# A routed two-layer block on one core: the second half's attention, its router and several helper steps put earlier in each engine's program

## The chip, the cores and the metric

The kernel runs on one core of one Trainium2 chip. The metric is the device time of one execution in microseconds (us); the number that counts is the median of several runs. A change of about 1% is the least that a measurement of this kernel can tell from no change.

## The reference

The input x has 4 sequences of 256 rows with 256 features; ctx has 4 x 256 x 64. Four residual steps follow one another, each on a layer-normalised copy:

```python
x = x + tanh(g_xattn[0]) * attn0(layernorm(x), ctx)       # sim = x' (kv'kv) with its own norm, softmax over 256
x = x + tanh(g_ffn[0])   * ffn0(layernorm(x))             # top-1 of 32 masked ternary 256x256 weights, times its probability
x = x + tanh(g_xattn[1]) * attn1(ctx, layernorm(x))       # top 76 of 256 of sim(ctx), sigmoid, symmetrised, mixed with x
x = x + tanh(g_ffn[1])   * ffn1(layernorm(x))             # 64 experts of width 64, top 8, plus a shared expert
```

In `attn0`, `ffn0` and `ffn1` each row depends on itself (and on ctx) alone. In `attn1` the 256 x 256 matrix of each sequence is added to its transpose, and this needs all 256 thresholds of the sequence.

## The kernel before

The 1024 rows are 8 tiles of 128 rows (t = 0..7), in two halves h = 0, 1 of four tiles. Each engine has a program that is written out by hand in a fixed order; semaphores tie them together. An engine that waits holds everything that stands behind the wait in its own program. VectorE is "DVE", ScalarE "ACT", GpSimd "POOL", SyncE "SP" and TensorE "PE" in the rows.

Front part (to about 123 us of the profiled execution), per half:

- `similarity`, `scale_rows`, `similarity_rows`, `softmax_rows`, `attend`: the first attention. `attend(h)` adds its result to X and asks GpSimd for the root of the variances (`rsqrt(r, n)`: POOL computes `rstd` for request r; each request is answered at its fixed place in POOL's program). `attended(h)` takes the answer.
- `router_x` (PE transposes), `router_rows` (ACT copies), `router(h)` (PE products), `choose(h)` (DVE top-1), `ranks`, `assign_spares`, `owners`, `assign_owners`, `owners_of`, `assign_slots`: every row gets a slot in a table of 12 x 128 rows, 32 rows an expert; an expert with more rows gets spare places. `set_owners(h)` writes which expert owns each of 15 spares.
- `scatter(h)` (POOL, indirect DMA) writes the rows to slots in DRAM, `load_rows(h)` (ACT's DMA queue) brings them back in expert order. `load_spares(h)` (SP) copies the owner's weights to each spare place: per spare one `value_load` of the owner's number and one DMA.
- `routed_x(h, p)` (PE transposes), `routed_rows(h, p)` (ACT copies to xT), `experts(h, p)` (PE), `expert_rows(h, p)` (ACT copies), `store_rows(h, p)` (DMA), for p = 0..5. Then `gather(h)` (POOL) brings each row its result, `weigh_rows` (ACT) weighs it and `add_rows` (POOL) adds it to X.
- Meanwhile DVE works through `find(n)`: n steps of a search for the 76th largest value of each row of `SIM`. A tile takes 19 steps (`MAX8` and `MATCH_REPLACE8` in turn), eight tiles 152. When a tile is through, `adjacency(t)` makes the thresholded matrix. `mask_weights(m)` multiplies the 32 masks into ternary weights, in 8 pieces.
- `rows_stats`, `rows_ask(0)` (request 4), `rows_affine(0)`, `mix_rows(0)` (ACT), `symmetric(0, k)` (PE: matrix plus transpose), `rows_mix(0)`, `rows_moments(0)` (request 5), `rows_normalise(0)`: the second attention of half 0 and the norm after it. `prep_x3t(0)`, `prep_logits(0)`, `top_find(0)`, `top_weigh(0)`, `prep_wt(0)`, `first_weights` make ready the last layer.
- `high_half(q)` (ACT) and `low_half(q)` (POOL) split the fp32 weights of expert pair q into two fp16 halves. `keep_busy(n)` gives PE n matmuls whose result nobody reads.

Main part: for half 0 and then half 1, one shared step and 32 pair steps (n = 0..32, and NS = 33 on). A step is `project` (12 matmuls of 512 columns), `silu_step`, `gate_step`, `weigh_step`, `high_step`, `low_step`, `down` (12 matmuls of 256 columns). Half 0's loop has half 1's later work in it at fixed values of n: `rows_stats` to `rows_normalise(1)`, `symmetric(1, k)`, `prep_x3t(1)`, `prep_logits(1)`, `lows(1)`, `top_find(1)`, `top_weigh(1)`, and at n = 32 `prep_wt(1)`. `final(h)` adds the accumulated result to X after the last `down` of a half, and SP writes it out.

## Time and profile before

| | us |
|---|---|
| median of 3 runs | 409.98 |
| lowest and highest | 407.95, 410.47 |
| the profiled execution's own time | 406.02 |
| its span, first to last instruction | 404.3 |
| TensorE matmul busy (share of the span) | 358.7 (89%) |
| VectorE busy | 272.6 (67%) |
| ScalarE busy | 181.1 (45%) |
| GpSimd busy | 163.0 (40%) |
| mean granted TensorE clock, share of full | 0.947 |

The span is read in three stretches: the front part up to about 123 us, where the engines wait for one another; half 0's loop of steps up to 268 us; half 1's loop to the end. The profiled execution is 3.96 us below the median.

### The profile page before, as it was taken

The numbers are of one execution on the slowest core, as the hardware profiler recorded it, in microseconds if no ns is written. First come the engines' busy times: TensorE is split into PE (matmuls) and PEld (weight loads), VectorE is DVE, ScalarE is ACT, GpSimd is POOL, SyncE is SP. The second block draws the span as 40 slices with busy tenths as digits, with TensorE's granted clock in tenths as the row PEclk, the third lists the DMA queues.
The fourth block names the chain that finished last, engine by engine and source line by source line (L and its number), as shares of the span: only waits on it lengthen the run. The fifth ranks groups of instructions, "written<-read, shape, count | busy, mean of one in ns | idle before, by whom it ended". The sixth has DMA issues, their size and how long they took to land. (4 is left out here: it accounts for less than half of the span.)

```text
span 404.3 us, 7694 instructions
## 1 busy us (share of the span) xinstructions
PE 358.7 (89%) x2419; PEld 217.4 (54%) x2419; DVE 272.6 (67%) x711; ACT 181.1 (45%) x354; POOL 163.0 (40%) x180
## 2 busy tenths in 40 slices
PE   8987928643977899999899999969999999999995
PEld 2755426312644365546466666645665656656563
DVE  3999896999376585999784484557555555555454
ACT  3477736624744446544645446533323233332331
POOL 6937542437551349978699677220000000000000
PEclk9996967785999899999999999999999999999999
DMA  7899964686701444445355442004121221212211
GB/s 186 139 258 218 197 208 149 221 263 217 233 17 51 128 137 131 130 131 195 132 190 174 159 153 73 25 29 146 61 78 58 72 71 58 78 56 74 77 53 52
DMA packets 50346, 51.31 MB, mean 127 GB/s; under 512 B 6732, under 2 KB 41484, under 8 KB 50318
## 3 DMA queue, kind: packets, MB, share of 16 engines
q1 hardware_dynamic: 34430, 38.08, 30.0%
q0 software_dynamic: 9216, 6.29, 9.1%
q10 hardware_dynamic: 6672, 6.59, 5.1%
q8 instruction: 14, 0.23, 0.2%
q14 instruction: 14, 0.11, 0.1%
HBM read 44.13 MB, written 7.08 MB: 127 GB/s over the span
## 5 line engine op out<-in xcount | busy, mean ns | idle before, releaser
L1047 PE MATMUL bank<-early,gu 128*128 128x512 f16 x768 | 177.7, 381 | 3.0 <-DVE arena L1608 3.0
L1047 PEld LDWEIGHTS bank<-early,gu 128*128 128x128 f16 (+1 forms) x768 | 75.0, 98 | 83.0 <-issue 4.4
L499 ACT ACTIVATE arena<-arena 128x512 f16<-128x512 f32 (+1 forms) x66 | 41.6, 631 | 134.6 <-DVE arena L1624 133.8
L1074 PE MATMUL bank<-dp,arena 128*128 128x256 f16 (+1 forms) x768 | 94.2, 273 | 1.1 <-POOL arena L457 0.7
L1074 PEld LDWEIGHTS bank<-dp,arena 128*128 128x128 f16 x768 | 74.7, 98 | 23.5 <-POOL arena L457 2.7
L1608 DVE TENSOR_TENSOR arena<-arena,bank 128x512 f32<-128x512 f32 x64 | 43.9, 686 | 56.7 <-PE bank L1047 40.2
L457 POOL TENSOR_TENSOR arena<-arena 128x512 f16<-128x512 f32 (+1 forms) x33 | 38.3, 1161 | 51.1 <-ACT arena L499 51.1
L1624 DVE TENSOR_TENSOR arena<-arena,early 128x512 f32<-128x512 f32 x64 | 48.4, 756 | 7.5 <-DVE arena L1608 2.7
L740 ACT ACTIVATE arena<-bank 128x512 f32<-128x512 f32 (+1 forms) x66 | 38.7, 588 | 17.5 <-PE bank L1047 17.4
L406 POOL TENSOR_TENSOR gu<-stage,gu 128x512 f16<-128x512 f32 x32 | 39.0, 1219 | 7.4 <-ACT dp L499 7.4
L1634 DVE TENSOR_TENSOR arena<-arena 128x512 f16<-128x512 f32 (+1 forms) x33 | 22.8, 691 | 24.5 <-ACT arena L499 24.5
L1206 DVE MAX8 t<-work 128x8 f32<-128x256 f32 x72 | 30.7, 426 | 2.0
L795 PE MATMUL bank<-ones 128*128 128x512 f16 x97 | 26.5, 420 | 1.8 <-DVE ones L1508 1.1
L407 POOL TENSOR_TENSOR dp<-stage,dp 128x256 f16<-128x256 f32 x32 | 27.5, 859 | 0.0
L1211 DVE MATCH_REPLACE8 work<-t,work 128x256 f32<-128x256 f32 x64 | 26.1, 408 | 0.0
L499 ACT ACTIVATE gu<-stage 128x512 f16<-128x512 f32 x32 | 19.7, 617 | 0.7 <-ACT arena L499 0.5
L975 PE MATMUL bank<-gu 128*32 128x256 f16 x256 | 12.0, 344 | 7.7 <-ACT gu L499 7.7
L795 PEld LDWEIGHTS bank<-ones 128*128 128x128 f16 x97 | 9.3, 104 | 16.0 <-issue 7.4
L499 ACT ACTIVATE arena<-bank 128x512 f32<-128x512 f32 (+1 forms) x18 | 10.7, 595 | 12.9 <-PE bank L975 7.0
L399 POOL TENSOR_TENSOR rstd<-var_in,minus_half 128x4 f32<-128x4 f32 x8 | 8.2, 1026 | 18.5 <-DVE var_in L1247 17.0
L1233 DVE BATCH_NORM_STATS2 bn<-X 128x6 f32<-128x256 f32 x32 | 11.8, 413 | 5.2 <-DMA X<-in_x 5.2
L420 POOL DMA_INDIRECT routed_rows<-arena,slot x8 | 10.1, 1265 | 8.9 <-DVE slot L1397 7.1
(184 smaller groups left out, 368.6 us busy)
## 6 DMA issues: line engine op xcount, KB each, us to landing
early<-token_weights SPq DMA_DIRECT2D x126, 128.0 KB, 2.9
stage<-in_gu_t SPq DMA_DIRECT2D x32, 256.0 KB
gu<-in_masks_t POOLq DMA_DIRECT2D x16, 256.0 KB, 22.5
stage<-in_dp_t SPq DMA_DIRECT2D x32, 128.0 KB
expert_rows<-arena ACTq DMA_DIRECT2D x12, 256.0 KB
dp<-gu SPq DMA_DIRECT2D x22, 128.0 KB, 2.3
routed_rows<-arena SPq DMA_DIRECT2D x1, 1536.0 KB, 17.5
arena<-routed_rows ACTq DMA_DIRECT2D x3, 512.0 KB, 5.1
```

Source lines behind the costliest of these rows:

```text
L406: nc.gpsimd.tensor_tensor(gu16[:, q, 1, :, :], stage_gu[s], gu16[:, q, 0, :, :], ALU.subtract)
L407: nc.gpsimd.tensor_tensor(dp16[:, q, 1, :], stage_dn[s], dp16[:, q, 0, :], ALU.subtract).then_inc(lo_ready, 1)
L457: nc.gpsimd.tensor_tensor(inter16[0:m, s, 1, :], inter[0:m, s, :], inter16[0:m, s, 0, :], ALU.subtract).then_inc(ilo_ready, 1)
L499: return nc.scalar.activation(dst, src, ACT.Copy, scale=scale)
L740: nc.scalar.activation(silu[0:m, s, :], ps_gate[s][0:m, :], ACT.Silu).then_inc(silu_ready, 1)
L795: mm(dst.rearrange("p (a b) -> p a b", a=4), ones16[:, :], ones16[:, None, :].to_broadcast([P, 4, P]), start=True, stop=True)
L1047: last = mm(dst[:, :], w, x16[:, h, b, c, :], start=(k == 0), stop=(k == 3 * C - 1))
L1074: last = mm(dst, inter16[0:m, s, a, k * P:(k + 1) * P], w, start=(q is None and j == 0 and k % 2 == 0), stop=True, skip_group_check=True)
L1206: last = steps(v.max(t8[:, t, :], src))
L1211: last = steps(v.match_replace(work[:, :], t8[:, t, :], src, NEG))
L1608: v.tensor_tensor(gated[0:m, s, :], silu[0:m, s, :], up, ALU.mult).then_inc(gated_ready, 1)
L1624: v.tensor_tensor(inter[0:m, s, :], gated[0:m, s, :], row, ALU.mult).then_inc(inter_ready, 1)
```

## The change

No operation of the computation is added or dropped; the program of every engine is reordered at some places. In words: on DVE `similarity_rows(1)` stands ahead of the mask products and `attend(1)` right behind them, and search steps are dealt out otherwise; on PE `router_x((2, 3))` and `router(1)` stand ahead of or behind the first expert group, the last transpose of it goes to another bank, `symmetric(0, 0)` stands among half 1's experts, and `keep_busy` counts change; on ACT `weigh_rows` of half 0 stands behind half 1's first two `routed_rows`, `load_rows(1)` ahead of two `high_half`; on POOL `rsqrt(4)` and `rsqrt(5)` stand ahead of `low_half`; SP reads all 15 owners before it waits for the masks; `rows_mix` and `rows_moments` of half 0 are merged tile by tile (`rows_mixed`); in half 0's loop `lows(1)`, `prep_logits(1)`, `top_find(1)` and `top_weigh(1)` come one step sooner; `final(1)` starts on two tiles when their bank is done.

```diff
@@ load_spares (SP)
                 sp.wait_ge(owner_set, h + 1)
+                owner = [sp.value_load(spare_e[0:1, h, j:j + 1], min_val=0, max_val=E0 - 1) for j in range(SPARE)]
                 sp.wait_ge(mask_ready, MB)
-                for j in range(SPARE):
-                    e = sp.value_load(spare_e[0:1, h, j:j + 1], min_val=0, max_val=E0 - 1)
+                for j, e in enumerate(owner):
@@ gpsimd
-            for q in range(4, 7):
-                low_half(q)
             rsqrt(4, HT)
+            low_half(4)
+            low_half(5)
+            rsqrt(5, HT)
+            low_half(6)
+            gather(1)
             low_half(7)
-            rsqrt(5, HT)
-            gather(1)
@@ scalar
+            softmax_rows(1)
             load_rows(0)
-            softmax_rows(1)
             routed_rows(0, 0)
             routed_rows(0, 1)
+            router_rows(1)
             expert_rows(0, 0)
             routed_rows(0, 2)
             store_rows(0, 0)
+            norm_rows(1, 4, 5)
...
+            load_rows(1)
             high_half(4)
             high_half(5)
-            load_rows(1)
-            weigh_rows(0, 1, 2, 3)
             routed_rows(1, 0)
             routed_rows(1, 1)
+            weigh_rows(0, 1)
             expert_rows(1, 0)
+            weigh_rows(2, 3)
...
             prep_rows(0)
             top_rows(0)
+            silu_step(0, 1, I1)
             prep_weights(0)
-            silu_step(0, 1, I1)
...
-                if n == 27:
+                if n == 26:
                     prep_rows(1)
-                if n == 30:
+                if n == 29:
                     top_rows(1)
@@ tensor
-                        pe.wait_ge(xnt_copied, 3)
+                        pe.wait_ge(sim_used, HT)
...
+                    if isinstance(n, int) and n == 2 * NS - 1 and k == HT // 2 - 1:
+                        last.then_inc(bank_done, 1)
...
+            symmetric(0, 0)
             experts(1, 0)
...
-            keep_busy(10, bank[0][:, :])
-            symmetric(0, 0)
+            keep_busy(6, bank[0][:, :])
             symmetric(0, 1)
-            keep_busy(14, bank[0][:, :])
+            keep_busy(24, bank[0][:, :])
             prep_x3t(0)
...
-                if n == 29:
+                if n == 28:
                     prep_logits(1)
@@ vector
-            find(2)
+            find(5)
             assign_spares(0)
             find(1)
             assign_owners(0)
             assign_slots(0)
             set_owners(0)
+            similarity_rows(1)
             for m in range(2, MB):
                 mask_weights(m)
-            similarity_rows(1)
+            attend(1)
             weights_of_rows(0)
-            find(4)
-            attend(1)
-            find(3)
+            find(2)
             attended(1)
-            find(6)
+            find(7)
             choose(1)
...
             thresholds(2)
+            find(2)
             rows_affine(0)
-            rows_mix(0)
-            rows_moments(0)
+            rows_mixed(0)
             find(3)
             rows_normalise(0)
...
+            def rows_mixed(h):
+
+                r = asked[0]
+                asked[0] += 1
+                rows_mark[1] = r
+                tiles = tiles_of(h)
+                done = {}
+                for t in tiles:
+                    rows_mix(h, t)
+                    done[t] = rows_mark[0]
+                    if t > tiles[0]:
+                        steps.need(done[t - 1])
+                        done[t - 1] = steps(moments(X[:, t - 1, :], t - 1))
...
+                dve.wait_ge(bank_done, 1) if h else dve.wait_ge(down_ready, NS)
                 for k in range(HT):
                     t = HT * h + k
+                    if h and k == HT // 2:
+                        dve.wait_ge(down_ready, 2 * NS)
...
-                if n == 27:
+                if n == 26:
                     lows(1)
+                if n == 29:
+                    top_find(1)
                 if n == 30:
-                    top_find(1)
-                if n == 31:
                     top_weigh(1)
```

On PE, the first expert groups of half 0. L896/L899 are `router_x`, L908/L911 `router`, L951/L954 `routed_x`, L975/L978 `experts`. Before:

```order
32 L951 MATMUL bank<-ident,arena 128x128 x16
33 L975 MATMUL bank<-gu 32x256 x32
34 L951 MATMUL bank<-ident,arena 128x128 x8
35 L975 MATMUL bank<-gu 32x256 x32
36 L951 MATMUL bank<-ident,arena 128x128 x8
37 L896 MATMUL bank<-ident,X 128x128 x8
38 L975 MATMUL bank<-gu 32x256 x32
39 L951 MATMUL bank<-ident,arena 128x128 x8
40 L908 MATMUL bank<-router_c,xn_t 128x32 x8
```

After:

```order
32 L954 MATMUL bank<-ident,arena 128x128 x16
33 L899 MATMUL bank<-ident,X 128x128 x8
34 L978 MATMUL bank<-gu 32x256 x32
35 L954 MATMUL bank<-ident,arena 128x128 x8
36 L911 MATMUL bank<-router_c,xn_t 128x32 x8
37 L978 MATMUL bank<-gu 32x256 x32
```

The router's transposes moved ahead of the first expert group, and its products ahead of the second.

On POOL, behind `add_rows` of half 0. L399/L400 is `rsqrt`, L406/L407 and L407/L408 the two instructions of `low_half`, L429/L430 `gather(1)`. Before:

```order
48 L406 TENSOR_TENSOR gu<-stage,gu 128x512
49 L407 TENSOR_TENSOR dp<-stage,dp 128x256
50 L406 TENSOR_TENSOR gu<-stage,gu 128x512
51 L407 TENSOR_TENSOR dp<-stage,dp 128x256
52 L406 TENSOR_TENSOR gu<-stage,gu 128x512
53 L407 TENSOR_TENSOR dp<-stage,dp 128x256
54 L399 TENSOR_TENSOR rstd<-var_in,minus_half 128x4
55 L406 TENSOR_TENSOR gu<-stage,gu 128x512
56 L407 TENSOR_TENSOR dp<-stage,dp 128x256
57 L399 TENSOR_TENSOR rstd<-var_in,minus_half 128x4
```

After:

```order
48 L400 TENSOR_TENSOR rstd<-var_in,minus_half 128x4
49 L407 TENSOR_TENSOR gu<-stage,gu 128x512
50 L408 TENSOR_TENSOR dp<-stage,dp 128x256
51 L407 TENSOR_TENSOR gu<-stage,gu 128x512
52 L408 TENSOR_TENSOR dp<-stage,dp 128x256
53 L400 TENSOR_TENSOR rstd<-var_in,minus_half 128x4
54 L407 TENSOR_TENSOR gu<-stage,gu 128x512
55 L408 TENSOR_TENSOR dp<-stage,dp 128x256
56 L430 DMA Z<-expert_rows,slot 128x256 x4
```

The first root moved ahead of three weight halves, the second ahead of two, so that one half now stands right behind it.

On ACT, at the start of half 1's experts. L615/L617 is `load_rows(1)`; `Z<-Z,tiny` is `weigh_rows`, `gu<-bank` is `routed_rows`, `arena<-bank` is `expert_rows`. Before:

```order
76 L615 DMA early<-routed_rows 128x4x512 x3
77 L499 ACTIVATE Z<-Z,tiny 128x256 x4
78 L499 ACTIVATE gu<-bank 128x1024 x2
79 L499 ACTIVATE arena<-bank 128x512
80 L499 ACTIVATE gu<-bank 128x1024
```

After:

```order
77 L501 ACTIVATE gu<-bank 128x1024 x2
78 L501 ACTIVATE Z<-Z,tiny 128x256 x2
79 L501 ACTIVATE arena<-bank 128x512
80 L501 ACTIVATE Z<-Z,tiny 128x256 x2
81 L501 ACTIVATE gu<-bank 128x1024
```

The copies that feed half 1's experts moved ahead of the weighing.

## Rows read from the trace of the kernel before

**Rows 1.** TensorE's waits over the whole span: us in total, times, longest.

```profile
PE bank L975 <- ACT gu L499: 7.9, 3, 6.3
...
PE bank L1023 <- DVE Z L1496: 4.4, 2, 3.2
```

**Rows 2.** Chain that ended last, half 1's loop: start us, us, what.

```profile
274.50 1.31 PE bank L1074 x12
275.81 2.59 PE bank L1047 x12
```

**Rows 3.** VectorE's waits in 38 to 119 us.

```profile
DVE mix L1441 <- POOL rstd L399: 5.9, 1, 5.9
DVE lg L1349 <- PE bank L908: 3.7, 1, 3.7
DVE X L1452 <- PE bank L996: 2.0, 2, 1.1
DVE spares L1367 <- PE bank L925: 1.4, 1, 1.4
```

**Rows 4.** VectorE's timeline, front part: start us, us, what, idle before it.

```profile
44.20 11.02 DVE L1504 TENSOR_TENSOR gu<-gu,tern 128x1024 f16<-128x1024 f16 x12
...
98.61 0.41 DVE L1233 BATCH_NORM_STATS2 bn<-X 128x6 f32<-128x256 f32 x1
...
103.39 0.24 DVE L1433 TENSOR_SCALAR var_in<-mv 128x4 f32<-128x4 f32 x1
...
110.91 0.23 DVE L1441 TENSOR_SCALAR mix<-rstd,k_mix 128x4 f32<-128x4 f32 x1 [5.91 <-POOL rstd L399]
...
116.90 0.17 DVE L1247 TENSOR_SCALAR var_in<-mv 128x4 f32<-128x4 f32 x1
...
118.31 1.46 DVE L1283 TENSOR_SCALAR XN<-X,mv,rstd 128x256 f32<-128x256 f32 x4
```

**Rows 5.** Costliest groups, the search steps: busy, mean ns, idle before.

```profile
L1206 DVE MAX8 t<-work 128x8 f32<-128x256 f32 x72 | 30.7, 426 | 2.0
...
L1211 DVE MATCH_REPLACE8 work<-t,work 128x256 f32<-128x256 f32 x64 | 26.1, 408 | 0.0
```

**Rows 6.** GpSimd's timeline: a weight half, and the root for request 4.

```profile
100.70 1.16 POOL L406 TENSOR_TENSOR gu<-stage,gu 128x512 f16<-128x512 f32 x1
...
109.83 1.05 POOL L399 TENSOR_TENSOR rstd<-var_in,minus_half 128x4 f32<-128x4 f32 x1
```

**Rows 7.** TensorE's timeline, end of the front part.

```profile
114.00 3.19 PE L795 MATMUL bank<-ones 128*128 128x512 f16 x14
119.08 1.40 PE L1006 MATMUL bank<-ident,XN 128*128 128x128 f32 x8 [1.90 <-DVE XN L1283]
...
133.40 4.22 PE L1047 MATMUL bank<-early,gu 128*128 128x512 f16 x12 [1.26 <-DVE arena L1608]
```

**Rows 8.** ScalarE's timeline.

```profile
84.03 0.60 ACT L499 ACTIVATE arena<-bank 128x512 f32<-128x512 f32 x1 [3.68 <-remote]
...
111.46 2.08 ACT L540 ACTIVATE Z<-X,mix 128x256 f32<-128x256 f32 x4 [1.92 <-DVE mix L1444]
...
130.60 1.28 ACT L740 ACT_TABLE_LOAD   x1
```

**Rows 9.** SyncE's DMA issues: spare weights of half 0, then token weights.

```profile
56.23 18.58 SPq L285 DMA_DIRECT2D dp<-gu  x15
...
131.95 4.99 SPq L332 DMA_DIRECT2D early<-token_weights  x8
```

**Rows 10.** Line L1504, all instructions: duration ns min/median/max.

```profile
L1504 DVE TENSOR_TENSOR gu<-gu,tern x16: 683/685/4402, 21.6 to 50.8; 128x1024 f16<-128x1024 f16 x16
```

**Rows 11.** VectorE's timeline, half 1's normalisation beside GpSimd's work.

```profile
236.99 3.06 DVE L1283 TENSOR_SCALAR XN<-X,mv,rstd 128x256 f32<-128x256 f32 x4 [0.31 <-POOL rstd L399]
```

**Rows 12.** Timelines at `prep_wt(1)` and at the end.

```profile
267.35 0.65 PE L1023 MATMUL bank<-ident,Z 128*65 128x128 f32 x4 [3.20 <-DVE Z L1496]
...
400.16 1.66 DVE L1641 SCALAR_TENSOR_TENSOR X<-bank,tg,X 128x256 f32<-128x256 f32 x4 [1.58 <-PE bank L1074]
```

More of the change, by code:

```diff
@@ L193, in flamingo_block @@
         ps_x3t = [bank[0], bank[7]], [bank[2], bank[1]]
-        ps_xr = [bank[1], bank[3], bank[1], bank[1]]
+        ps_xr = [bank[1], bank[3], bank[1], bank[7]]
         ps_down = [bank[0], bank[7]]
@@ L248, in flamingo_block @@
         logits1_copied = sem("logits1_copied")
+        bank_done = sem("bank_done")
         x_d = x.rearrange("b s d -> (b s) d").rearrange("(t p) d -> p t d", p=P)
@@ L664, in _ @@
             store_rows(0, 1)
-            router_rows(1)
-            norm_rows(1, 4, 5)
+            norm_rows(1, 6, 7)
             expert_rows(0, 2)
@@ L669, in _ @@
             store_rows(0, 2)
-            norm_rows(1, 6, 7)
+            router_exp(1)
             expert_rows(0, 3)
@@ L703, in _ @@
             store_rows(1, 3)
-            high_half(6)
             expert_rows(1, 4)
@@ L709, in _ @@
             mix_rows(0)
+            high_half(6)
             high_half(7)
@@ L1114, in _ @@
             routed_x(0, 1)
+            router_x((2, 3))
             experts(0, 0)
             routed_x(0, 2)
+            router(1)
             experts(0, 1)
             routed_x(0, 3)
-            router_x((2, 3))
             experts(0, 2)
             routed_x(0, 4)
-            router(1)
             experts(0, 3, 0)
@@ L1453, in rows_mix @@
                                                                 ALU.mult, ALU.add))
+            def rows_mixed(h):
[10 more added lines that the diff above has]
+                        done[t - 1] = steps(moments(X[:, t - 1, :], t - 1))
+                steps.need(done[t])
+                done[t] = steps(moments(X[:, t, :], t))
+                for t in tiles:
+                    steps.need(done[t])
+                    m = steps(v.bn_aggr(mv[:, t, :], bn[:, t, :]))
+                steps.need(m)
+                v.tensor_scalar(var_in[:, r, :], mv[:, HT * h:HT * h + HT, 1], 1.0, EPS, ALU.mult, ALU.add
+                                ).then_inc(var_ready, 1)
             def rows_normalise(h):
```

2 lines of the change are left out of this document (removed).

## The prediction

> **What bounds the kernel now.** I read TensorE's waits first, then the chain that ended last, then VectorE's waits and its timeline over the front part. From 123 us on TensorE is nearly always busy: a step of half 1's loop is 2.59 us of projection and 1.31 us of down, 3.90 us together, and the chain runs through these alone [rows 2]. No edit touches that pace. What can be won is waiting: one wait of 3.20 us in the middle, where TensorE needs the token weights of half 1 (`prep_wt(1)`) [rows 12], the tail behind the last matmul, and the front part, whose end is the start of the steps. TensorE's largest single wait in front is 6.3 us for ScalarE [rows 1], but to end it is worth nothing by itself, for what ends the front part is VectorE: TensorE waits 1.90 us for the normalised rows at 119.08 although it has 3.19 us of filler just ahead [rows 7]. So the front part is costed on VectorE. From 44.20 on it has masks, search steps and norms without a hole until 98.61, except where rows 3 say so: 1.4 us for the ranks, 3.7 for the router's logits, 5.9 for the root of request 4 and 2.0 for the symmetric products, 13.0 us together [rows 3, 4].
>
> **Half 0's ranks.** Three more search steps stand ahead of `assign_spares(0)`. A step is 0.43 or 0.41 us plus a short value load, about 0.49 as they follow one another [rows 5], so 1.4 us of wait become 1.4 us of work: gain 1.4. The slots come 0.1 to 0.2 late, taken as nothing.
>
> **Second router sooner.** With `similarity_rows(1)` (about 1.6 us) ahead, the masks start near 46.0 and end near 57.0 in place of 55.2 [rows 4]. `attend(1)` follows at once, so its rows stand in X at 59.1, some 2 us sooner than before. TensorE, which then has just transposed the first routed rows, transposes X (0.6 us a group) and starts the experts about when it did before; the logits come near 65.4. VectorE reaches `choose(1)` at about 65.7: the 3.7 us are gone. The new wait is for `ranks(1)`: three expert groups stand ahead of it on TensorE, so it ends near 69.9 and VectorE, there at 69.1, waits some 1.1. Net gain 2.6. Slots of half 1 near 73.4, before 77.4.
>
> **Spare owners.** Fifteen loads with their register reads take 18.58 us, 1.24 each; plain issues of this queue take 4.99 for eight, 0.62 each [rows 9]. Read ahead, the copies of half 0 take some 9.3 us behind the masks and end near 67, ahead of the need at about 72. For half 1 the reads can't hide, because the owners come near 74.5 and the masks are long done: 9.3 of reads, 9.3 of copies, landing at about 96. Half 1's experts need them at 96 to 97. Worth nothing here on the path, and a wait of up to 1 us on TensorE is covered, since ScalarE's mix isn't wanted before 103.
>
> **Gather, weighing, and half 1's experts.** The results of half 0 are stored near 77, gathered from about 80 and added to X by about 93; VectorE, with the same search work to do, comes to `rows_stats(0)` only at about 95 (98.61 before [rows 4]), so the moved `weigh_rows` costs nothing; the cover is 2 us. Half 1's experts start near 88 in place of 97.9 and are through at about 99.5, ahead of the mix.
>
> **GpSimd's root first.** The request goes out at 103.39, the root starts at 109.83, since `low_half(6)` stands ahead and waits for a ScalarE copy that stands behind the experts [rows 4, 6]. Put first, it answers 1.05 us after the request. VectorE meanwhile has four search steps and a threshold matrix. Gain 5.9.
>
> **Symmetric products and merged mix.** The first product is done among the experts, the second by 103.4. Then ScalarE sets the pace: 2.08 us for four tiles [rows 8]. From the affine step to the request for root 5 it was 110.91 to 116.90, 6.0 us [rows 4]; now I get 4.5. Gain 1.5 of the 2.0.
>
> **Sum in front.** 1.4 + 2.6 + 5.9 + 1.5 = 11.4. Two more search steps stand ahead of `rows_normalise(0)` than before (81, not 79): minus 1.0. This gives 10.4; a walk through the timeline by durations gives 9.9 to 10.4, with the normalised rows near 108.5 and the longer filler (24 instructions for 14, some 5.2 us at the rate of 3.19 for 14 [rows 7]) ending about then.
>
> **What VectorE and GpSimd do to each other.** One mask product took 4.40 us where the median is 0.69: it lasted through two weight halves of GpSimd [rows 10]. Half 1's normalisation took 3.06 us for four tiles beside GpSimd's work, half 0's took 1.46 [rows 4, 11]. The new order brings such neighbours: the choice of half 1 beside `low_rows`, the matrix of tile 2 beside `add_rows`, the affine step beside `low_half(4)` and `(5)`, and above all `rows_normalise(0)` right beside `low_half(6)`, which was done before. From below nothing, from above 1.6 (normalise, 3.06 less 1.46) plus one stall of 3.7 (4.40 less 0.69). I take 1.1 for normalise, since its first tiles meet one or two of those instructions, and 1.3 for the other three together: minus 2.4. Front gain **8.0**. The Trainium skill, "SBUF — State Buffer", Who interferes with whom, says that a VectorE instruction with two SBUF inputs, or one in a two-port mode, and a GpSimd instruction that reads SBUF exclude each other, and that the later one blocks for the other's whole instruction. By that rule each of the four meetings would cost up to one GpSimd instruction of 1.16 us, 4.6 in all, and the front would gain 5.8; the 4.40 us row shows more than one instruction's worth in one stall, so the trace agrees with the exclusion and not with its length.
>
> **Start of the steps.** `silu_step(0)` now pays its table load of 1.28 us [rows 8] while ScalarE had been waiting for the transposed weights. Its silu is ready some 2.5 us sooner, the weights copy 0.4 later, and the step that started at 133.40 after a wait of 1.26 [rows 7] can start behind `first_weights`, at 132.6: gain 0.8. That step took 4.22 us, against 2.59 for the same work, at a granted clock of 1.2 GHz in part; if the shorter hole holds 2.4 GHz, 1.6 more. I leave this out, as a hole of 1.2 us remains.
>
> **Middle.** Everything from `prep_logits(1)` to `top_weigh(1)` comes one step, 3.9 us, sooner; 1.75 us of logits only change places. `top_weigh(1)` then ends near 263.4, TensorE is there at 264.1: gain **3.2**, with 0.7 to spare. What is late next is nothing, the token weights shift along. `prep_rows(1)` one step sooner holds `silu_step(27)` until the transposes are copied, about 4 us; the double buffer has room for one step, so none is charged; without it 1 us.
>
> **Tail.** Two tiles of `final(1)` run while TensorE does the last six matmuls. `final` was 1.66 us [rows 12] behind the last matmul, now half of it; the outputs are issued one after the other, so 0.65 is gained. Extra wait instruction: none that shows.
>
> **Sum.** 8.0 + 0.8 + 3.2 + 0.65 = 12.65. The profiled execution took 406.02, so 393.4 by its own time; it lies 3.96 under the median of 409.98, against which the forecast is 409.98 - 12.65 = **397.3 us**.
>
> **Rivals.**
> - Full gain: no stall between VectorE and GpSimd, and the clock holds in the first step. Front 10.4, start 2.4, so 16.65 gained: 393.3. For it: search steps ran at 0.43 beside weight halves. Against: rows 10 and 11. Chance 0.17.
> - The gather chain takes VectorE's place. ScalarE sat 3.68 us before the last expert copy of half 0 on something that no engine of this core explains [rows 8]; if that stays and transfers (gather, rows of half 1, spare copies) crowd one another, X is complete near 99 instead of 93, and the front gains 4 less: 401.3. The Trainium skill, "DMA: Bandwidth & Descriptors", Issuing engines are not separate DMA queues, says that all queues share the same engines; no row here separates what each lost. Chance 0.20.
> - The longer filler is the bound: 24 matmuls at 1.2 GHz take 10.3 us instead of 5.2, and the transposes wait for them, 4 to 5 us: 401.8. It needs a clock that fell in the 1.7 us hole ahead of the second product; the hole of 1.90 us before 119.08 [rows 7] left it at full speed. Chance 0.07.
> - The order does not do what it says: VectorE's freed waits come back behind another, such as the mask products, and only the middle and tail gain, 3.85: 406.1. Chance 0.04.
> - Slower: TensorE starts the steps at 1.2 GHz and stays there, as the half step at 133.40 did for a while [rows 7]. Every step would cost 3.9 us more; past 3.3 steps the whole gain is gone, at five it is 397.3 + 19.5 = 416.8. Against it: the next projection of the same length in the trace is back at its full pace of 2.59, and so are all behind it [rows 2]. Chance 0.02.
>
> The forecast itself has 0.50. The range reaches from the full gain to the two cases near 401.5, with 1 us on the low and 2 on the high side for what the median itself moves: 392.3 to 403.5. A time of under 405.9 is faster by over 1%; that holds for all but the last two cases and some luck of the median: faster 0.92, within 1% 0.05, slower 0.03.
>
> **What would show it.** VectorE: no wait for the root and none for logits, about 1 us for ranks, `rows_normalise(0)` starting at 108 to 111. TensorE: the first `prep_x3t` 7 to 10 us sooner, no wait at L1023's successor near 260 us, 3.90 a step as before. SyncE: copies 0.62 apart. GpSimd: the first root straight behind its request. Wrong it would be if VectorE showed a new wait for `rows_added`, or the transposes started behind the filler.

## The result, and the profile after

| | before | after |
|---|---|---|
| median | 410.23 (407.95 to 411.04, 4 runs) | 393.28 (392.48 to 394.04, 4 runs) |
| ratio, 95% interval | | 0.9595 (0.9549 to 0.9642) |
| the profiled execution's own time, span | 406.02, 404.3 | 392.48, 390.7 |
| mean granted TensorE clock | 0.947 | 0.965 |

The changed kernel is faster, and 393.28 lies inside the range of 392.3 to 403.5, 4.0 below the forecast of 397.3. The forecast was a gain of 12.65 us, made from one execution; the same execution pair gained 13.54. The medians, 16.95 apart, gained more than either trace. The unaltered changed kernel, measured a second time (told below), gave 11.2 us by medians and a ratio of 0.9675 (0.962 to 0.9731), which is 13.2 of 407.39; ratios here leave out a kernel's runs that lie more than 1.5% above its fastest. So the gain that this pair of traces supports is 13.5. What the medians add or take away is at least in part the clock, below; the later measurements were also made on three different chips, and no run here separates chip from execution.

To compare traces I cut each span at TensorE's own rows: the first product of `ranks(0)`, the first transpose of `prep_x3t(0)`, the projection behind `first_weights`, the first down step, `prep_wt(1)`, and the last down step. "Front" is from the first of these to the second, and so on; the tail is what is left of the span.

| | ranks at | front | start | first projection | half 0 | half 1 | tail | span |
|---|---|---|---|---|---|---|---|---|
| before | 40.41 | 78.67 | 14.32 | 4.16 | 129.79 | 131.29 | 5.65 | 404.3 |
| after | 41.17 | 69.12 | 13.33 | 2.69 | 127.22 | 132.22 | 4.99 | 390.7 |
| difference | +0.76 | -9.55 | -0.99 | -1.47 | -2.57 | +0.93 | -0.66 | -13.6 |

VectorE's waits in the front part after the change (columns: what waited for what, us in total, times, longest), the answer to [rows 3]:

```profile
DVE X L1457 <- ACT Z L542: 0.7, 1, 0.7
```

The waits for ranks, logits and the root are gone altogether; of 13.0 us one of 0.7 is left. VectorE's timeline shows what that bought (columns: start, duration, operation, and in brackets the idle time before it and what ended it), against [rows 4]:

```profile
99.69 0.17 DVE L1438 TENSOR_SCALAR var_in<-mv 128x4 f32<-128x4 f32 x1
...
102.01 0.26 DVE L1446 TENSOR_SCALAR mix<-rstd,k_mix 128x4 f32<-128x4 f32 x1
102.31 0.59 DVE L1448 SCALAR_TENSOR_TENSOR mix<-mv,mix 128x4 f32<-128x4 f32 x1
...
103.64 0.98 DVE L1457 SCALAR_TENSOR_TENSOR X<-bank,k_mix,Z 128x256 f32<-128x256 f32 x2 [0.67 <-ACT Z L542]
...
107.03 0.17 DVE L1479 TENSOR_SCALAR var_in<-mv 128x4 f32<-128x4 f32 x1
...
108.42 2.47 DVE L1288 TENSOR_SCALAR XN<-X,mv,rstd 128x256 f32<-128x256 f32 x4
```

The request for root 4 goes out at 99.69 instead of 103.39, the affine step is at 102.0 instead of 110.91, the request for root 5 at 107.03 instead of 116.90, and the normalised rows start at 108.42, inside the 108 to 111 that was forecast. They take 2.47 us, not 1.46 as in [rows 4]. GpSimd's timeline shows the neighbour:

```profile
99.94 1.05 POOL L400 TENSOR_TENSOR rstd<-var_in,minus_half 128x4 f32<-128x4 f32 x1 [4.88 <-DVE var_in L1438]
...
107.28 1.01 POOL L400 TENSOR_TENSOR rstd<-var_in,minus_half 128x4 f32<-128x4 f32 x1 [2.65 <-DVE var_in L1479]
108.26 1.14 POOL L407 TENSOR_TENSOR gu<-stage,gu 128x512 f16<-128x512 f32 x1
109.37 0.71 POOL L408 TENSOR_TENSOR dp<-stage,dp 128x256 f16<-128x256 f32 x1
```

Both roots now start within 0.25 us of their request, and `low_half(6)` runs while VectorE normalises: 1.01 us too much, where the sum had 1.1.

TensorE's timeline, against [rows 7, 12]:

```profile
103.14 5.34 PE L798 MATMUL bank<-ones 128*128 128x512 f16 x24
110.29 1.32 PE L1009 MATMUL bank<-ident,XN 128*128 128x128 f32 x8 [1.80 <-DVE XN L1288]
...
119.98 0.65 PE L1026 MATMUL bank<-ident,Z 128*65 128x128 f32 x4 [1.32 <-DVE Z L1523]
121.65 1.07 PE L1062 MATMUL bank<-early,ident 65*64 65x512 f32 x2 [1.02 <-ACT early L501]
...
123.62 2.76 PE L1050 MATMUL bank<-early,gu 128*128 128x512 f16 x12
...
180.73 2.75 PE L1050 MATMUL bank<-early,gu 128*128 128x512 f16 x12 [0.68 <-DVE arena L1634]
...
253.53 0.60 PE L1026 MATMUL bank<-ident,Z 128*65 128x128 f32 x4
...
265.45 1.48 PE L1077 MATMUL bank<-shared_dn,arena 64*128 64x256 f16 x12 [0.91 <-DVE X L1669]
```

The reader is to see four things. The transposes (L1009) come at 110.29 instead of 119.08, 8.8 us sooner, and still wait for VectorE with an idle hole ahead. The projection at 123.62 took 2.76 where its counterpart took 4.22. `prep_wt(1)` at 253.53 has no bracket any more: the 3.20 us are gone. And two waits are new, 0.68 at 180.73 and 0.91 at 265.45, neither of which the prediction had.

SyncE's timeline, against [rows 9]:

```profile
58.11 11.53 SPq L286 DMA_DIRECT2D dp<-gu  x15
...
83.25 5.10 SPq L286 DMA_DIRECT2D arena<-gu  x8
88.49 4.44 SPq L286 DMA_DIRECT2D dp<-gu  x7
```

Fifteen spare copies of half 0 take 11.53 us, 0.77 each, not the 0.62 of plain issues and not 1.24. Half 1's fifteen, in the two lower rows, take 9.7 together.

### The profile page after: what moved, and what is told of

It is laid out like the page before. It is cut to its first block and busy times, and to the rows that moved or that the text cites. A ratio compares the mean times of both kernels' runs of the same rounds, so it can differ in the third digit from the quotient of the medians.

```text
span 390.7 us, 7704 instructions
## 1 busy us (share of the span) xinstructions
PE 357.3 (91%) x2425; PEld 219.2 (56%) x2425; DVE 275.5 (71%) x711; ACT 179.8 (46%) x354; POOL 162.2 (42%) x180
## 5 line engine op out<-in xcount | busy, mean ns | idle before, releaser
L407 POOL TENSOR_TENSOR gu<-stage,gu 128x512 f16<-128x512 f32 x32 | 39.0, 1219 | 0.0
L408 POOL TENSOR_TENSOR dp<-stage,dp 128x256 f16<-128x256 f32 x32 | 27.5, 859 | 0.0
L400 POOL TENSOR_TENSOR rstd<-var_in,minus_half 128x4 f32<-128x4 f32 x8 | 8.2, 1026 | 24.4 <-DVE var_in L1252 15.4
L501 ACT ACTIVATE gu<-bank 128x1024 f16<-128x1024 f16 x12 | 12.1, 1021 | 10.0 <-PE bank L954 8.3
L1531 DVE TENSOR_TENSOR gu<-gu,tern 128x1024 f16<-128x1024 f16 x16 | 13.6, 914 | 0.9 <-DMA gu<-in_masks_t 0.9
```

What stands on the lines that cost most here:

```text
L407: nc.gpsimd.tensor_tensor(gu16[:, q, 1, :, :], stage_gu[s], gu16[:, q, 0, :, :], ALU.subtract)
L408: nc.gpsimd.tensor_tensor(dp16[:, q, 1, :], stage_dn[s], dp16[:, q, 0, :], ALU.subtract).then_inc(lo_ready, 1)
L501: return nc.scalar.activation(dst, src, ACT.Copy, scale=scale)
```

## The experiments

Twelve runs follow: eleven variants, and the changed kernel once more (after_again). Times are medians; the ratio is to the kernel before, run beside it. The medians of the kernel before in the four measurements were 410.23, 411.15, 407.23 and 407.39, so kernels of different measurements are compared by ratio or stretch by stretch. The columns from "front" on come from one profiled execution of each, cut as above.

| | time | ratio (95%) | front | start | first | half 0 | half 1 | span |
|---|---|---|---|---|---|---|---|---|
| changed kernel | 393.28 | 0.9595 (0.9549 to 0.9642) | 69.12 | 13.33 | 2.69 | 127.22 | 132.22 | 390.7 |
| u_root | 395.6 | 0.9624 (0.9578 to 0.967) | 70.70 | 13.48 | 4.17 | 127.21 | 132.31 | 394.4 |
| u_spares | 401.55 | 0.9793 (0.9732 to 0.9854) | 76.54 | 13.33 | 2.69 | 127.25 | 132.18 | 398.8 |
| u_silu | 397.25 | 0.9665 (0.9611 to 0.9718) | 69.34 | 14.41 | 4.92 | 127.25 | 132.42 | 396.3 |
| u_middle | 397.31 | 0.9695 (0.9623 to 0.9768) | 68.91 | 13.33 | 2.69 | 130.57 | 132.97 | 395.9 |
| b_root | 410.55 | 1.0071 (1.0027 to 1.0114) | 77.49 | 14.42 | 5.08 | 129.76 | 132.82 | 405.6 |
| x_gather | 395.96 | 0.9732 (0.9647 to 0.9817) | 67.88 | 15.73 | 4.67 | 127.20 | 132.35 | 394.3 |
| x_final | 393.86 | 0.9665 (0.9583 to 0.9748) | 68.85 | 15.13 | 3.99 | 127.85 | 131.24 | 394.1 |
| x_filler14 | 394.7 | 0.9695 (0.9618 to 0.9772) | 69.39 | 14.16 | 2.69 | 127.84 | 132.21 | 394.2 |
| after_again | 396.23 | 0.9675 (0.962 to 0.9731) | 70.06 | 15.12 | 3.95 | 127.20 | 132.34 | 395.3 |
| x_busy | 394.42 | 0.9712 (0.9676 to 0.9747) | 69.62 | 13.33 | 2.69 | 128.25 | 132.19 | 392.3 |
| x_calm | 397.64 | 0.9783 (0.9738 to 0.9828) | 68.15 | 17.00 | 5.07 | 127.19 | 132.20 | 395.0 |
| x_best | 395.43 | 0.9679 (0.9618 to 0.974) | 69.54 | 14.90 | 2.68 | 128.13 | 131.23 | 392.2 |

How well a stretch repeats can be read from this table. Six of these kernels are alike up to the first transpose (changed kernel, u_silu, u_middle, x_final, after_again, x_busy), and their fronts are 68.85 to 70.06 long: a difference of about 1 us in the front is hardly more than that spread. Half 1 repeats within 0.3 us where nothing in it was changed and the clock held. Half 0 is 127.2 long in most, but 127.8 to 128.3 in four kernels whose edits lie outside it. By the ratios, of the four edits undone only u_spares lies clear of the changed kernel's interval; the prices of the other three rest on the rows of one profile each.

### Four edits undone, one at a time

**u_root**: GpSimd's root for request 4 behind three weight halves again. `rsqrt(5)` and `gather(1)` stay ahead of `low_half(7)`, which they were not in the kernel before.

```diff
@@ gpsimd, in the changed kernel
+            for q in range(4, 7):
+                low_half(q)
             rsqrt(4, HT)
-            low_half(4)
-            low_half(5)
             rsqrt(5, HT)
-            low_half(6)
             gather(1)
             low_half(7)
@@ scalar
             store_rows(1, 3)
+            high_half(6)
             expert_rows(1, 4)
...
             mix_rows(0)
-            high_half(6)
             high_half(7)
```

> The changed kernel with GpSimd's two roots put back behind the weight halves, and ScalarE's copy for pair 6 back among the experts. Theory A (VectorE's program is what ends the front part, and the root answered late was the largest hole in it): the first root waits for low_half(6), whose ScalarE copy now comes at about 97 us, so the root is done near 103 to 104 in place of 101; a hole of 1 to 2 us on VectorE ahead of the affine step, less some 1 us that normalise wins back without low_half beside it. Span 390.7 + 0 to 1.5, some 391.5. Rival B (the 5.9 us were the root's own, whatever else moves): the hole comes back at 5 to 6 us, span 396.

Measured: the wait for the root is 3.7, between the two theories, and the front is longer by 1.58 only. VectorE's timeline of this kernel:

```profile
105.56 0.23 DVE L1445 TENSOR_SCALAR mix<-rstd,k_mix 128x4 f32<-128x4 f32 x1 [3.68 <-POOL rstd L400]
105.82 0.16 DVE L1447 SCALAR_TENSOR_TENSOR mix<-mv,mix 128x4 f32<-128x4 f32 x1
...
111.51 1.47 DVE L1287 TENSOR_SCALAR XN<-X,mv,rstd 128x256 f32<-128x256 f32 x4
```

With the halves done early nothing of GpSimd's lies beside the affine step (0.16 for 0.59) or the normalise (1.47 for 2.47). So 3.7 of wait bought 1.4 of undisturbed VectorE, and of the price of 1.58 some 1 us lies within the spread of the front. Another 1.5 us is in the first projection, 4.17 for 2.69, and that, as the later runs show, is not to be booked to this edit.

**u_spares**: SyncE reads each owner just before its copy again.

```diff
@@ load_spares (SP), in the changed kernel
-                owner = [sp.value_load(spare_e[0:1, h, j:j + 1], min_val=0, max_val=E0 - 1) for j in range(SPARE)]
                 sp.wait_ge(mask_ready, MB)
-                for j, e in enumerate(owner):
+                for j in range(SPARE):
+                    e = sp.value_load(spare_e[0:1, h, j:j + 1], min_val=0, max_val=E0 - 1)
```

> The changed kernel with each spare owner read just ahead of its copy, as before. Theory A (read ahead is worth nothing of its own): the copies of half 0 take 18.6 us from 58.1, land at 79, TensorE waits 7 us more at the spare experts, but VectorE reaches the row statistics only at 94.9 and absorbs up to 3 us; half 0's rows are complete near 102 in place of 95, so 7 us late, 3 to 5 us on the span: 394 to 396. Rival B (the wait is swallowed by the rest of the front): no change, 390.7 within 0.5.

Measured: the front is 7.42 us longer, by far the largest price of the four. The waits of TensorE and of VectorE and the queue of SyncE in this kernel:

```profile
PE bank L978 <- DMA dp<-gu: 12.6, 2, 9.6
...
DVE spare_e L1408 <- PE bank L939: 7.8, 1, 7.8
...
59.35 20.15 SPq L286 DMA_DIRECT2D dp<-gu  x15
```

The copies take 20.15 us and end at 79.5, TensorE stands 9.61 us in front of `experts(0, 4)` and the product of `owners_of(1)` (L939), 32x16 elements large, stands behind it in TensorE's program; VectorE's `set_owners(1)` waits 7.8 us for that product. In the changed kernel the same place costs TensorE 1.28. Both theories missed: the span is 398.8, beyond the 394 to 396 of theory A, for VectorE absorbed nothing. It comes to `rows_stats(0)` at 103.0 instead of 94.9, since it stood in that wait itself.

**u_silu**: `prep_weights(0)` ahead of `silu_step(0)` again.

```diff
@@ scalar, in the changed kernel
             top_rows(0)
-            silu_step(0, 1, I1)
             prep_weights(0)
+            silu_step(0, 1, I1)
```

> The changed kernel with the copy of the transposed token weights back ahead of the shared silu. Theory A (the table load is hidden in a wait, and the shorter hole keeps TensorE's clock at 2.4 GHz): the second projection starts 0.8 to 1.0 later and takes 4.2 instead of 2.7 us, span 390.7 + 2.4 = 393.1. Rival B (the clock held for another reason, such as the longer filler ahead of it): only the start moves, span 391.6.

Measured: start +1.08 and first projection +2.23. The 1.08 agrees with the 0.8 of the sum. The 2.23 is clock (4.99 us for work that takes 2.75 at 2.4 GHz), and I had taken it as confirmed by this run that the longer hole brings it; after the runs below I do not.

**u_middle**: `lows(1)`, `prep_logits(1)`, `top_find(1)` and `top_weigh(1)` one step later again.

```diff
@@ tensor (the same by one in scalar and vector), in the changed kernel
-                if n == 28:
+                if n == 29:
                     prep_logits(1)
```

> The changed kernel with half 1's logits, top-8 search and weights back at their old steps of half 0's loop. Theory A: TensorE's wait of 3.2 us for the token weights returns, while the wait of 0.9 us for final(0) goes, since the last stretch shifts: span 390.7 + 3.2 - 0.9 = 393.0. Rival B (the 0.9 us wait has nothing to do with it): span 393.9.

Measured: half 0 +3.35, half 1 +0.75. TensorE's timeline shows what happened in half 1:

```profile
257.98 0.65 PE L1026 MATMUL bank<-ident,Z 128*65 128x128 f32 x4 [3.20 <-DVE Z L1523]
258.47 2.34 PE L1077 MATMUL bank<-dp,arena 128*128 128x256 f16 x12
260.60 2.31 PE L1036 MATMUL bank<-early,shared 128*128 128x512 f16 x6
```

The 3.20 us wait is back, to the hundredth. The 0.91 us wait for `final(0)` is gone, for TensorE is later; but the two groups behind the hole ran at 2.34 and 2.31 us instead of 1.47 and 1.46, 1.7 us of clock. In the kernel before the same hole of 3.20 [rows 12] left the clock at full speed: the group behind it took 1.47. A first hint that a hole does not decide by itself.

### The root alone

**b_root**: the kernel before, with GpSimd's part behind `add_rows` in the changed kernel's order (`rsqrt(4)` ahead of `low_half(4)`, `rsqrt(5)` ahead of `low_half(6)`, `gather(1)` ahead of `low_half(7)`) and `high_half(6)` behind `mix_rows(0)`, nothing else.

> The kernel before with one edit: GpSimd answers request 4 ahead of low_half(4) and request 5 ahead of low_half(6), and ScalarE's high_half(6) stands behind mix_rows(0). Theory A (the waits are layered): the 5.9 us wait for the root goes, but half 1's experts of the old order hold TensorE's symmetric products and ScalarE's mix until about 109.6 to 110.5 us, so VectorE waits for them instead; the front is shorter by 1 to 3 us, and the time is about 407 to 409 beside 410 to 411. Theory B (my prediction's sum, in which the root alone was worth 5.9): about 404.5 to 405.

Measured: the front is 1.18 us shorter, and the kernel is not faster at all (ratio 1.0027 to 1.0114). VectorE's timeline:

```profile
105.76 1.13 DVE L1442 TENSOR_SCALAR mix<-rstd,k_mix 128x4 f32<-128x4 f32 x1
...
110.22 0.88 DVE L1453 SCALAR_TENSOR_TENSOR X<-bank,k_mix,Z 128x256 f32<-128x256 f32 x2 [2.63 <-PE bank L997]
111.97 0.88 DVE L1453 SCALAR_TENSOR_TENSOR X<-bank,k_mix,Z 128x256 f32<-128x256 f32 x2 [0.88 <-PE bank L997]
...
116.01 2.14 DVE L1284 TENSOR_SCALAR XN<-X,mv,rstd 128x256 f32<-128x256 f32 x3
```

The affine step is 5.2 us sooner (105.76 for 110.91), the normalise 2.3 (116.01 for 118.31), the transposes 1.2 (117.86 for 119.08). Between them the wait for the symmetric products, which stand behind half 1's experts, grew from 2.0 [rows 3] to 3.5, and two stalls beside weight halves came in, at the affine step and at the normalise. What was left was lost again where the clock fell (first projection 5.08, and 1.5 in half 1, where the transposes behind the 3.19 us hole took 1.12 instead of 0.65). Theory A (layered waits) holds for the front, at the low end of its 1 to 3 us; the gain in time that it still expected did not come.

### Moving GpSimd's weight half out of the way

**x_gather** and **x_calm**:

```diff
@@ gpsimd, x_gather
             rsqrt(5, HT)
-            low_half(6)
             gather(1)
+            low_half(6)
             low_half(7)
@@ gpsimd, x_calm: as x_gather, and
             gather(1)
+            pool.wait_ge(top_ready, 1)
             low_half(6)
```

> The changed kernel with low_half(6) behind gather(1) on GpSimd, so that nothing of GpSimd's arithmetic stands beside rows_normalise(0). Theory A (GpSimd's half blocks VectorE): the four normalising instructions fall from 2.47 us to about 1.46, the transposes start 1.0 sooner, 392.3 by the median. Theory B (their price lies in something else, such as the DMA traffic or ScalarE's copies at 105.98 to 108.6): 2.47 stays and the time stays at 393.3. If GpSimd's indirect DMAs hold VectorE as much, 2.47 or more stays as well.

> The changed kernel with low_half(6) and (7) on GpSimd behind gather(1) and behind a wait for the row maxima (top_ready), so that they stand beside neither rows_normalise(0) nor the four-element scaling in top_find(0), which took 1.47 us in place of 0.34 when low_half(6) was only moved behind gather(1). Theory A: normalise 1.46, the scaling 0.34, transposes 1.0 to 1.3 sooner and the start stretch as in the changed kernel (13.3), so 1.1 less in span at equal clock. Theory B (the stall moves on again, to the expert softmax or the first gate steps): the start stretch grows by 0.7 to 1.2 and nothing is gained.

Measured in x_gather, on VectorE:

```profile
108.41 1.46 DVE L1288 TENSOR_SCALAR XN<-X,mv,rstd 128x256 f32<-128x256 f32 x4
...
115.75 1.47 DVE L1505 TENSOR_SCALAR tiny<-top 128x4 f32<-128x4 f32 x1
```

and in x_calm:

```profile
107.81 1.46 DVE L1289 TENSOR_SCALAR XN<-X,mv,rstd 128x256 f32<-128x256 f32 x4
...
116.01 0.63 DVE L1517 SCALAR_TENSOR_TENSOR Z<-Z 128x64 f32<-128x64 f32 x1
...
117.21 1.18 DVE L1517 SCALAR_TENSOR_TENSOR Z<-Z 128x64 f32<-128x64 f32 x1
```

In both, normalise falls to 1.46, as theory A said of the cause: it is the weight half that made it 2.47. (GpSimd's indirect DMAs ran beside it instead, as in the kernel before, where it took 1.46 too.) But the stall moves. In x_gather it hits a scaling of four elements a row, 1.47 us, which took 0.34 in the changed kernel and 0.17 in x_calm. GpSimd's rows of x_gather show how long it was held: through the rest of one instruction and the whole of the next.

```profile
115.42 1.15 POOL L407 TENSOR_TENSOR gu<-stage,gu 128x512 f16<-128x512 f32 x1
116.53 0.66 POOL L408 TENSOR_TENSOR dp<-stage,dp 128x256 f16<-128x256 f32 x1
```

TensorE's hole ahead of `prep_wt(0)` grows from 1.32 to 2.43 by it, so the front's gain of 1.24 is given back in the start stretch; the rest of what that stretch and the next lost is clock. In x_calm the stall hits the four masked sums of the softmax: 0.63, 0.70, 1.18 and 0.69 where 0.21 to 0.23 is usual, 2.3 us in all, more than the 1.0 that it saved in front, and here too the clock fell behind the longer hole, of 3.11. For the gain at the end, theory B was right in both.

### The wait for final(0)

**x_final**:

```diff
@@ vector, in the changed kernel
             low_step(NS, 0, I1)
-            gate_up(NS + 1, 1)
             final(0)
+            gate_up(NS + 1, 1)
```

> The changed kernel with final(0) ahead of the gate and weigh steps of n = NS + 1 on VectorE. TensorE waited 0.91 us at 265.45 us for final(0), which stood behind two instructions that VectorE could run only late. Theory A: final(0) runs at about 262.4, the 0.91 goes, and the time is 0.9 lower, 392.4. Theory B: what is late is the whole VectorE chain of the shared step (it waited 1.99 us for ScalarE and 0.60 for the token weights' DMA just before), so the wait moves to the down step behind it and the time is unchanged, 393.3.

Measured: half 1 is 131.24 against 132.22, so the wait is gone, 0.98 us, and didn't move to the down steps behind it: theory A. It came from order alone. `final(0)`, whose last input was complete at 261.9 in the changed kernel, stood behind the gate and weigh steps until 263.74. The median did not show the 0.98: this kernel's four times are 395.83, 391.69, 395.75 and 391.96, two pairs 4 us apart. That opened the last question.

### The clock at the first projection

**x_filler14** (24 filler matmuls made 14), **after_again** (the changed kernel, unaltered), **x_busy** and **x_best** (x_busy, x_calm and x_final together):

```diff
@@ tensor, x_busy
             pair_step(0, 0, 0)
+            keep_busy(5, bank[0][:, :])
             prep_wt(0)
+            keep_busy(4, bank[0][:, :])
             first_weights(0, I1)
```

> The changed kernel with keep_busy(14) in place of keep_busy(24) ahead of prep_x3t(0). The filler ends 2.2 us sooner, so TensorE idles about 4.0 us ahead of the transposes instead of 1.80, as it did with the root put back (4.01 us, and the first projection then took 4.17). Theory A (the long filler is what keeps the granted clock through the first projection): the projection at 121.65 or so takes 4.2 instead of 2.7, 1.5 us lost, 394.8. Theory B (the earlier end of the front part, not the filler, did it): the time stays at 393.3.

> The changed kernel, unaltered, as the base for the three variants that run beside it. Theory A (one execution holds the granted clock through the first weights and projections at about 122 us and another doesn't, by chance): its times fall into two groups some 2 to 4 us apart, as an unaltered front part did in the run with final(0) moved (391.7 and 392.0 against 395.8 and 395.8). Theory B: they lie within 1.5 us, as in the first measurement (392.5 to 394.0), and the spread there had come from that variant.

> The changed kernel with five filler matmuls ahead of prep_wt(0) and four behind it, at 0.22 us each, where TensorE had waited 1.32 and 1.02 us. Theory A (the clock at the first projection depends on TensorE's holes just before): the weights' products stay at 1.07 and 1.12 us and the first projection at 2.7 in every execution; the slow group of times goes, and the median is 392 to 393, 1 to 2 below the changed kernel beside it. Theory B (what makes the clock fall lies elsewhere, in the first 110 us): two groups remain, and the median does not move.

> All together: low_half(6) and (7) behind the row maxima (minus 1.1), the fillers around prep_wt(0), and final(0) ahead of the gate step of n = NS + 1 (minus 0.9). Theory A: span 388 to 389, median 389.5 to 391, about 2 to 3 below the changed kernel beside it. Theory B (the gains overlap, or the filler delays what waits for it): above 391.5.

Measured first, the two profiles of one program. x_final's is the changed kernel's up to 262 us. TensorE's timeline in x_final:

```profile
120.59 0.65 PE L1026 MATMUL bank<-ident,Z 128*65 128x128 f32 x4 [1.32 <-DVE Z L1523]
122.26 1.97 PE L1062 MATMUL bank<-early,ident 65*64 65x512 f32 x2 [1.03 <-ACT early L501]
124.16 2.08 PE L1062 MATMUL bank<-early,pick 65*128 65x512 f32 x2
126.03 4.06 PE L1050 MATMUL bank<-early,gu 128*128 128x512 f16 x12
```

The holes ahead, 1.32 and 1.03, are those of the changed kernel's first profile, 1.32 and 1.02. There the weights' products took 1.07 and 1.12 and the projection 2.76. The stretches of the trace by 4 us (columns: window, length, TensorE busy and number of instructions, granted clock, share of the DMA engines, GB/s) say it directly. In x_final:

```profile
120.00:124.00 4.00, 2.39 (x6) 0.73 0.14 37
124.00:128.00 4.00, 4.00 (x8) 0.50 0.31 116
```

and in the first profile of the changed kernel:

```profile
120.00:124.00 4.00, 2.98 (x10) 1.00 0.13 37
124.00:128.00 4.00, 4.00 (x25) 1.00 0.42 152
```

So one program, with the same two holes, is granted 1.2 GHz from about 122 us in one execution and 2.4 in another, and it costs 3.1 us (start 15.13 for 13.33, first 3.99 for 2.69). The two were not alike in all that came before: the hole ahead of the transposes was 0.78 in x_final and 1.80 in the first profile. In the profiled execution of after_again (397.09) that hole is 1.80 too, and what follows is as in x_final: holes of 1.31 and 1.02, products of 1.97 and 2.08, a projection of 4.02. Theory A of after_again holds in that the clock there differs from execution to execution; what decides it is open, and these profiles are of different chips. x_final's four times, on one chip, do lie in two pairs. The "two groups" that theory A named for after_again did not come: the six times are 390.92, 394.11, 395.37, 397.09, 397.73 and 400.77, spread wider than this place explains. Another place is the start: `ranks(0)` came between 40.43 and 42.96 in the kernels of the changed order, whose programs are alike up to there.

x_busy closed the two holes to 0.24 and 0.16 us:

```profile
119.02 1.24 PE L798 MATMUL bank<-ones 128*128 128x512 f16 x5
120.50 0.65 PE L1026 MATMUL bank<-ident,Z 128*65 128x128 f32 x4 [0.24 <-DVE Z L1525]
...
122.17 1.07 PE L1062 MATMUL bank<-early,ident 65*64 65x512 f32 x2 [0.16 <-ACT early L501]
```

Its profile holds the clock, and its six times lie within 2.0 us (394.02 to 396.01), where even the three lowest of after_again span 4.5. That is what theory A said of the spread, with few runs behind it. The gain that it named is not shown: the median is 1.8 below that of after_again's six times, but 0.3 above that of its three lowest, the lowest time is 3.1 above after_again's lowest, and the ratios' intervals overlap (0.9676 to 0.9747 against 0.962 to 0.9731). So it looks steadier, and is not shown to be faster. In its profile half 0 is 1.0 longer, 0.73 of it one new wait for GpSimd at 159 us. Why, is open.

x_filler14 does not decide its question. The first projection took 2.75, not the 4.2 of theory A. The hole ahead of the transposes was 2.99 us, and the clock was down right behind it (0.70 and 0.50 in the windows 112 to 120), with the logits' products at 3.68 instead of 2.00. But u_middle had its clock down at the same place behind the very hole of 1.80 of the changed kernel, so one execution can't be read as an effect of the filler.

x_best: span 392.2, median 395.43, past the 391.5 that theory B named. `final(0)` gave its 1.0 (half 1 131.23), x_calm's stalls took 2.3 as before. There is no version here that is shown to beat the changed kernel. x_calm is shown to be slower: 0.9738 to 0.9828, against 0.962 to 0.9731 for the changed kernel beside it.

## Why the prediction was right, and where it was not

**The total.** Forecast 12.65 from one execution, measured 13.54 from one. Of this 1.47 is the clock of the first projection, which the sum left out; like for like it is 12.65 against 12.1, with 0.8 and 0.2 more than forecast in front and start, and 0.6 and 0.9 less in the two halves. The waits that were to go went, so it is right by mechanism and size, though the price of two single edits in it was wrong. Against the medians the forecast was 4.0 high: the base was the median of before, 4 us above its profiled execution, and the median after was only 0.8 above its own. The step "it lies 3.96 under the median, against which the forecast is 397.3" assumed that this distance is carried over. It isn't a property of the kernel: the changed kernel, measured again, had a median 5.3 above its lowest time. That the median came so far below the forecast is therefore luck.

**Front, forecast 8.0, measured 8.79 of time at the transposes** (9.55 less a start 0.76 later, which no edit explains). The waits for ranks, logits and root went, as said; not even the 1.1 us for `ranks(1)` came. VectorE reached `rows_stats(0)` first at 94.9 (forecast 95). The terms for the ranks (1.4), the second router (2.6) and the merged mix (1.5) were not tried one at a time; they rest on the waits that are gone from VectorE's rows.

**"Gain 5.9" for the root, the step that failed as a price.** Undone in the new order the edit is worth 1.58 in the front, of which the spread of fronts leaves about 1 open; made alone in the old order 1.18, and nothing in the time. The term was right as a piece of a sum in which the symmetric products and half 1's experts were also brought forward, and wrong as the value of the edit.

**"Worth nothing here on the path" for the spare owners: wrong.** By the prediction's own figures the copies without the edit, from about 57 at 1.24 each, would have ended near 75.6, 3.6 past the 72 at which it had them wanted. It asked only whether the copies with the edit are in time, and never priced the new order without it. In the kernel before TensorE waits 1.25 at this place, in u_spares 9.61. VectorE's `set_owners(1)` hangs, through one small product in TensorE's program, on the expert group that needs the spares. Reading ahead holds off 7.42 us. Copies cost 0.77 each, where I had 0.62.

**Start, forecast 0.8: measured 0.99**, and 1.08 when undone. **The first projection**, left out at 1.6, came as 1.47. It was rightly left out: x_final and after_again lack it, with the same program up to there. That it came is luck.

**Middle, forecast 3.2: measured 2.57.** The 3.20 went, and u_middle brings exactly it back. "What is late next is nothing" was wrong twice. At 180.73 TensorE waits 0.68: VectorE's rows show why.

```profile
178.02 1.07 DVE L1448 SCALAR_TENSOR_TENSOR mix<-mv,mix 128x4 f32<-128x4 f32 x1
179.02 0.16 DVE L1449 TENSOR_SCALAR mix<-mix 128x4 f32<-128x4 f32 x1
179.09 0.90 DVE L1234 SCALAR_TENSOR_TENSOR SIM<-SIM,t,XN 128x256 f32<-128x256 f32 x1
```

With the search steps dealt out otherwise, a threshold matrix (L1234) falls into the same step as half 1's affine step, ahead of the gate that TensorE wants; before, it came a step later. The 1.07 of the first row was there in the kernel before too; what is new is the matrix, 0.90 and not its usual 0.48, for it too stood beside a weight half. u_middle has the same wait of 0.68, so it is not from the moved logits and top-8 search. And at 265.45 the wait for `final(0)`, 0.91, took the place of part of the gain. That wait I could have read from the old trace, where `final(0)` ended at 278.05 and its user started at 278.34: it had 0.3 to spare, and the shift used it up (in u_middle, without the shift, the wait is not there).

**Tail, forecast 0.65: measured 0.66.**

**VectorE beside GpSimd, forecast 2.4: measured 2.2.** Normalise lost 1.01 (forecast 1.1). The other three meetings lost 1.2 (forecast 1.3): 0.69 for 0.24 in `assign_spares(1)` beside `low_rows`, 0.82 for 0.48 in the matrix of tile 2, 0.59 for 0.17 in the affine step. The Trainium skill, "SBUF — State Buffer", Who interferes with whom, was weighed there: exclusion for one GpSimd instruction. In x_calm each of the four stalled sums ended within 0.1 us of the end of one GpSimd instruction, which agrees. In x_gather the scaling took 1.47, 1.3 more than alone, and was held through the rest of one instruction and the whole of the next. So this row, like the 4.40 us of [rows 10], agrees with the exclusion and not with its length.

**Rivals.** The full gain (393.3) gives the median almost to the hundredth, for another reason than its own: its stalls-free front did not happen. The gather chain and the clock for good did not come. Nor did the filler: in all eleven profiles of the changed order with 24 of them they took 5.34 us, the rate of the full clock.

## What to carry to other kernels

A wait's length is not an edit's value: where waits are layered, as here, one edit made alone won nothing, and one that was "off the path" was worth 7.4 us once the others were in; cost each edit in the order in which it will run. When a stall between two engines is taken away, ask which instruction stands beside the disturbing one next: here it moved twice. In x_calm it cost 2.3 us on four small sums beside two weight halves, where four large instructions beside one had lost 1.0. When one profiled execution is compared with a median, check first whether the same program's executions differ at one place; here the clock behind a 1 us hole did, by 3 us.

## What the runs showed of the hardware

- Two executions of one program, with holes of 1.32 and 1.02 us in one and 1.31 and 1.02 in the other, were granted 1.00 and 0.50 of the clock right behind them. Holes of 3.20 and 3.19 us left it at full speed in one kernel and not in two others, and a hole of 2.03 left it at full speed in x_best, where one of 1.80 in u_middle did not. No hole length here decides it by itself; with them closed to 0.24 and 0.16 us the one profile taken held the clock.
- GpSimd's weight half delays some VectorE instructions and not others. Beside it, search steps ran at their usual 0.43 and 0.41, and the mask-out steps in x_calm at 0.21; a four-element scaling took 1.47 for 0.17, a masked sum 1.18 for 0.22. The Trainium skill, "SBUF — State Buffer", Who interferes with whom, says that an instruction with at most one SBUF input, outside the two-port modes, does not contend; the search steps agree. What I had not expected is that the size of the VectorE instruction does not matter: the stalls ended with a GpSimd instruction, so the one on four elements a row (1.3 too long) was longer than the one on 256 in the first normalised tile of the changed kernel (1.13 for 0.40).
- Beside GpSimd's indirect DMAs the normalise took 1.46 us in x_gather, x_calm and the kernel before. Its third tile took 0.51 where the others took 0.39 to 0.41, so they cost it at most 0.1. No run here has it without them.
- On SyncE a register read between two DMA issues is dear: 20.15 us for fifteen pairs against 11.53 with the reads ahead, 0.57 more for each.
